# Last layer of a graph network: 256 by 256 buckets, parts summed by the matmul, edge one-hots of eight tiles in one comparison

## The reference

```python
E, N, D, H = 200000, 6250, 32, 32
h = jnp.maximum(_layernorm(x, axis=-1), 0.0)
x = x + _L0_gnn_ref(h, edge_index, edge_attr_3, ...)      # three spline convolutions
h = jnp.maximum(_layernorm(x, axis=-1), 0.0)
# the last layer, inputs = h, e = edge_weight1
ex1 = e * x[src]
ex2 = e * x[dst]
mi = jnp.zeros_like(x).at[dst].add(ex1)
mo = jnp.zeros_like(x).at[src].add(ex2)
h = jnp.concatenate([mi, mo, x], axis=1)
h = jnp.tanh(h @ W1 + b1)      # four dense layers with tanh
```

## Time and profile before

| | us |
|---|---|
| median of 3 runs | 11384.52 |
| lowest, highest | 11377.37, 11390.43 |
| profiled execution: span | 11351.5 |
| median minus span | 33.0 |
| stretch of the last layer's loop | 2450 |

### The profile page before, as it was taken

The page is one execution under the profiler, slowest core; times in us unless marked ns, Lnnn a source line. Parts: engine busy times, 40 slices in busy tenths (PEclk is TensorE's granted clock), DMA queues, the critical chain, the costliest instruction groups (busy, mean ns, idle before and its releaser), DMA issues. The chain is left out here.

```text
span 11351.5 us, 410865 instructions
## 1 busy us (share of the span) xinstructions
PE 8343.0 (73%) x149059; PEld 7488.9 (66%) x149060; DVE 7972.5 (70%) x18151; ACT 4364.6 (38%) x11249; POOL 6850.3 (60%) x6842
## 2 busy tenths in 40 slices
PE   6666666666574566565679959898987788888888
PEld 6566655555463555555568847777776688888886
DVE  5577777776574444444458848888887788888887
ACT  0010000000352333333346624444444566666665
POOL 0277777777334777777777717777775334343333
PEclk6555555555555787787789969999999777777777
DMA  1033333332102333333332212222221344444432
GB/s 39 15 75 67 68 68 67 67 68 61 23 9 62 112 111 111 111 115 109 115 103 82 77 29 62 62 62 62 62 62 52 111 127 126 127 126 128 126 129 96
DMA packets 825177, 932.53 MB, mean 82 GB/s; under 512 B 336620, under 2 KB 581924, under 8 KB 824590
## 3 DMA queue, kind: packets, MB, share of 16 engines
q1 hardware_dynamic: 641290, 726.84, 22.9%
q0 software_dynamic: 183808, 204.63, 7.2%
HBM read 610.68 MB, written 134.61 MB: 66 GB/s over the span
## 5 line engine op out<-in xcount | busy, mean ns | idle before, releaser
L765 POOL DMA_INDIRECT edges_by_rank<-rank_stage,rank_idx x1568 | 1821.5, 1162 | 505.2 <-issue 475.8
L1427 POOL DMA_INDIRECT c_near_ranked<-h_rows,c_idx x1568 | 1664.9, 1062 | 477.7 <-issue 477.1
L1552 ACT ACTIVATE c_products<-c_pa 125x512 f32<-125x512 f32 x2368 | 1222.6, 603 | 1794.7 <-PE c_pa L1596 1778.7
L1879 POOL DMA_INDIRECT edges_b<-c_send_rows,c_send_idx x1184 | 1310.1, 1106 | 396.1 <-issue 355.0
L1596 PE MATMUL c_pa<-c_near_apart,c_basis 32*125 32x128 f32 x18944 | 744.9, 294 | 1013.5 <-DVE c_near_apart L1515 911.3
L289 PE MATMUL acc_s<-hot_col,hot_row 128*123 128x78 f16 x3136 | 757.0, 410 | 956.2 <-ACT start_table L721 839.9
L2527 PE MATMUL acc_mi_mo<-msg,hot_e 128*128 128x32 bf16 x11328 | 1364.5, 191 | 115.1 <-DVE hot_e L2406 99.8
L1596 PEld LDWEIGHTS c_pa<-c_near_apart,c_basis 32*125 32x125 f32 x18944 | 638.1, 195 | 1132.2 <-issue 1132.2
L289 PEld LDWEIGHTS acc_s<-hot_col,hot_row 128*123 128x123 f16 x3136 | 718.8, 320 | 990.7 <-issue 853.6
L2527 PE MATMUL acc_mi_mo<-msg_rest,hot_e 128*128 128x32 bf16 x11328 | 1338.0, 182 | 0.0
L2527 PE MATMUL acc_mi_mo<-msg_low,hot_e 128*128 128x32 bf16 x11328 | 1336.9, 182 | 0.0
(11 more groups left out here) (402 smaller groups left out, 21082.3 us busy)
## 6 DMA issues: line engine op xcount, KB each, us to landing
own_d<-hparts SPq DMA_DIRECT2D x1888, 96.0 KB
rows<-local_rows SPq DMA_DIRECT2D x472, 256.0 KB, 3.9
hi_rows_in<-hi_rows SPq DMA_DIRECT2D x392, 256.0 KB
c_dst_rows_in<-dst_rows SPq DMA_DIRECT2D x148, 512.0 KB
near_by_rank<-c_near_ranked SPq DMA_DIRECT2D x98, 768.0 KB
rows_both<-hi_rows SPq DMA_DIRECT2D x196, 196.0 KB
near_h<-c_near_h SPq DMA_DIRECT2D x74, 512.0 KB
c_near<-near_h SPq DMA_DIRECT2D x148, 256.0 KB, 2.7
```

Source lines behind the costliest of these rows:

```text
L765: pool.indirect_dma_start(g.ranked, bass.IndirectOffsetOnAxis(idx[:, r, q:q + 1], 0), stage[:, r, q, :], None, bounds_check=last_rank, oob ...
L1427: pool.indirect_dma_start(near[:, b, q, :], None, g.h1_rows, bass.IndirectOffsetOnAxis(idx[:, b, q:q + 1], 0), bounds_check=last_node, oob ...
L1552: last = act.activation(by_round[:, half, r, rnd], pa[0:K3, r, 0:TR * P].rearrange("p (f e) -> p f e", f=width), ACT.Copy)
L1879: pool.indirect_dma_start(g.edges_b, bass.IndirectOffsetOnAxis(sending.idx[:, n, q:q + 1], 0), sending.rows[:, n, q, :], None, bounds_chec ...
```

## The change

Target blocks have 256 nodes as source blocks have: 25 x 25 = 625 buckets. The worst case then needs NT = 2192 tiles, 274 chunks of 8, and `chunks_for` no longer rounds to pairs of 16. The table holds two column offsets per tile, ready for use.

In the last layer both sides have 2 blocks of 128 nodes. The gather runs 12 matmuls of 32 columns per tile instead of 6 of 96: the three parts are accumulated into the same 32 columns, so the bank holds all 8 tiles of a chunk and VectorE's reduction is gone. VectorE multiplies by the weights straight from the bank and also takes off the upper halves; GpSimd has nothing to do. The edge one-hots of 8 tiles and one side are made by one comparison of two tensors, `local` (the numbers of the edges, 8 tiles side by side) and `numbers` (the node numbers, each 8 times), in float16 with the tile innermost. The layout is [node, tile], so `add_up` reads its stationary operand with a step of 8 elements. There are 12 matmuls per tile in `add_up` instead of 18. All buffers hold whole chunks, doubled. TensorE gathers one half of a chunk (4 tiles), then adds up one half of the chunk before it, twice per chunk. In sorting, the one-hot of the target block has 27 entries instead of 14.

```diff
-SRC_SB, DST_SB = 256, 512
-SRC_SHIFT, DST_SHIFT = 8, 9
+SRC_SB, DST_SB = 256, 256
+SRC_SHIFT, DST_SHIFT = 8, 8
...
-    step = 2 * CH
-    return -(-tiles // step) * 2
+    return -(-tiles // CH)
...
-ND1 = ND + 1
+ND1 = NBLK * P // DST_SB + 1
...
+            st.add(dve.tensor_scalar(block_of[:, :, 0], count_b[:, :], float(DST_SB // P * F), None, ALU.mult))
+            st.do(dve.tensor_scalar(block_of[:, :, 1], count_a[:, :], float(SRC_SB // P * F), None, ALU.mult))
...
-        hot_e = sb1("hot_e3", [P, 2, G, DST_SB + SRC_SB], BF16)
+        hot_e = sb1("hot_e3", [P, 2, 2, DST_SB, SH], BF16)
+        numbers, local = sb1("node_numbers3", [P, DST_SB, SH], F16), sb1("local_nodes3", [P, 2, NT], F16)
...
+                with sp.Fori(0, TURNS - 1) as i:
+                    for half in range(2):
+                        sp.wait_ge(s_hot, i * 2 + (half + 1))
+                        sp.wait_ge(s_source, i * 2 + (half + 1))
+                        bring_rows(i + 1, half)
+                        sp.wait_ge(s_gat, i * 4 + (half + 1) * 2)
+                        bring_blocks(i + 1, half)
...
+                def edge_hots(i, half, side):
+
+                    dve.tensor_tensor(hot_e[:, half, side, :, :],
+                                      local[:, side, ds(i * (2 * SH) + half * SH, SH)].unsqueeze(1)
+                                      .to_broadcast([P, DST_SB, SH]), numbers[:, :, :], ALU.is_equal)
...
+                def chunk(i, half, first, follows):
+                    if not first:
+                        dve.wait_ge(s_used, i * 2 + (half - 1))
+                    times_weight(i, half, 0)
+                    for side in range(2):
+                        edge_hots(i, half, side)
+                    if follows:
+                        dve.wait_ge(s_row[1 - half], i * 32 + (half + 1) * 32)
+                        for j in range(NJ):
+                            hot = node_hot(1 - half, j)
+                        hot.then_inc(s_hot, 1)
+                    times_weight(i, half, 1)
+                    split_rest(i, half)
+                    split_low(i, half)
...
+                def gather(i, half, h, waits):
+
+                    if waits:
+                        pe.wait_ge(s_read, i * 4 + (half * 2 + h))
+                    for q in range(h * Q, (h + 1) * Q):
+                        for side, hot, own in ((0, hot_s, own_s), (1, hot_d, own_d)):
+                            at = (q * 2 + side) * F
+                            for n in range(NJ * 3):
+                                last = pe.matmul(pg[:, at:at + F], hot[:, half, n // 3, q * P:(q + 1) * P],
+                                                 own[:, half, q, n * F:(n + 1) * F],
+                                                 start=(n == 0), stop=(n == NJ * 3 - 1))
                     last.then_inc(s_gat, 1)
...
+                                    last = pe.matmul(acc[:, ds(cols[q * 2 + side] + (col + j * F), F)],
+                                                     hot_e[:, half, side, j * P:(j + 1) * P, q],
+                                                     part[:, half, q, side * F:(side + 1) * F],
+                                                     start=False, stop=True, skip_group_check=True)
...
+                def chunk(i, half, last):
+
+                    ready(i, half)
+                    cols = blocks_of(last, 1 - half)
+                    for h in range(2):
+                        gather(i, half, h, True)
+                        if h == 0:
+                            pe.wait_ge(s_low, i * 2 + half)
+                        add_up(last, 1 - half, h, cols)
```

More of the change, by code:

```diff
@@ L2299, in second_layer @@
         acc = c_ps.enter_context(nc.psum_tensor("acc_mi_mo", [P, 7 * 512], F32))
[L2301 to L2305 removed]
+        own_d = sb1("own_d3", [P, 2, SH, NJ * 3 * F], BF16)
@@ L2319, in _, with bring_rows @@
             def _(sp):
[L2320 removed]
+                def bring_rows(i, half):
                     for kind in range(2):
                         sp.dma_start(rows[:, half, kind, :],
[L2323 to L2332 removed]
@@ new lines, in _ @@
+                dve.tensor_copy(numbers[:, :, :], g.iota16[:, :].unsqueeze(2).to_broadcast([P, DST_SB, SH]))
+                for side, column in ((0, 1), (1, 0)):
+                    last = dve.tensor_copy(local[:, side, :], g.edges[:, :, column])
+                last.then_inc(s_ready, 1)
+                dve.wait_ge(s_ready, 1)
+                dve.wait_ge(s_row[0], 32)
+                for j in range(NJ):
+                    hot = node_hot(0, j)
+                hot.then_inc(s_hot, 1)
+                chunk(0, 0, True, True)
@@ L2420, in _ @@
+                chunk(0, 1, True, True)
+                with dve.Fori(1, TURNS - 1) as i:
+                    chunk(i, 0, False, True)
+                    chunk(i, 1, False, True)
+                chunk(TURNS - 1, 0, False, True)
+                chunk(TURNS - 1, 1, False, False)
             @block.scalar
             def _(act):
-                def take_blocks(n, b):
-                    both = load_values(nc, ACTE, g.table_b[0:1, ds(n * G, G)], NA * 16 - 1)
-                    for q in range(G):
-                        a = both[q] >> 4
-                        last = act.activation(own_s[:, b, q, :], hparts[:, ds(a * (NJS * 3 * F), NJS * 3 * F)], ACT.Copy)
-                    last.then_inc(s_own, 1)
@@ L2487, in _ @@
+                act.wait_ge(s_minus, 1)
+                for half in range(2):
+                    act.wait_ge(s_row[half], 32)
+                    sources(0, half)
+                with act.Fori(1, TURNS) as i:
+                    for half in range(2):
+                        act.wait_ge(s_row[half], i * 32 + 32)
+                        act.wait_ge(s_gat, i * 4 + (half - 1) * 2)
+                        sources(i, half)
             @block.tensor
@@ L2535, in two_chunks @@
-                def two_chunks(i, more):
-                    for m in range(2 * NPAIR):
-                        if m + AHEAD < 2 * NPAIR or more:
-                            gather(i, m + AHEAD)
-                        if m % 4 == 0:
-                            both = load_values(nc, PE, g.table_b[0:1, ds(i * (2 * SH) + 2 * m, 8)], NA * 16 - 1)
-                        add_up(i, m, both)
-                for m in range(AHEAD):
-                    gather(0, m)
-                with pe.Fori(0, LOOP - 1) as i:
-                    two_chunks(i, True)
@@ new lines, in chunk @@
+                def chunk(i, half, last):
[6 more added lines that the diff above has]
+                        add_up(last, 1 - half, h, cols)
+                ready(0, 0)
+                for h in range(2):
+                    gather(0, 0, h, h > 0)
+                chunk(0, 1, 0)
@@ L2550, in second_layer @@
+                with pe.Fori(1, TURNS) as i:
+                    chunk(i, 0, i - 1)
+                    chunk(i, 1, i)
+                cols = blocks_of(TURNS - 1, 1)
+                pe.wait_ge(s_low, NC)
+                for h in range(2):
+                    add_up(TURNS - 1, 1, h, cols)
         bufs.close()
```

266 lines of the change are left out of this document (77 added, 189 removed).

## The result

| | us |
|---|---|
| kernel before, median of 4 (lowest, highest) | 11380.94 (11377.21, 11390.43) |
| changed kernel, median of 4 (lowest, highest) | 11494.99 (11491.21, 11505.03) |
| ratio, 95% interval | 1.0102 [1.0089, 1.0114] |
| forecast | 11,560 (11,050 to 11,830), slower |

The changed kernel is 1.0% slower, 114 us. The profiled execution is its longest of the four, 11505.03 us with a span of 11503.2.

The account below looks back on a forecast made before the run. TensorE was to bound the last loop: 2.6 + 1.3 + 0.3 + 5.3 = 9.5 us a chunk, 274 chunks +153 us, +24 outside, so +177 on 11384.5: 11,560 us, range 11,050 to 11,830.

Parts of the forecast that it names:

- 8.94 us: Last loop: time per chunk at which 274 chunks would equal the present 2450 us; 8.85 with the side costs.
- adding up: TensorE's chunk in the last layer: 96 matmuls of `add_up` at 55 ns, slowed by the step of 8 elements, 5.3 us.
- table load and waits: TensorE's chunk: 16 numbers at 80 ns, 1.3 us at the chunk's head, plus four waits estimated at 0.3 us.
- Not covered: Claim that TensorE's table load, 1.3 us at the head of each chunk, runs beside no other TensorE work.
- What lies beside it: Last loop: VectorE 6.0 us a chunk, ScalarE 6.4, SyncE 6.6, all hidden below 9.5; if TensorE were free, about 7.6.
- load of 8 numbers 0.6: SyncE's table load per chunk in the last loop, taken as 0.6 us of its 6.6 us sum.
- the rival: The step costs nothing: adding up 3.2 to 4.1 us, chunk about 8.0, 11,150 us, faster; chance 0.20.
- Outside the loop: Stages beside the last loop: transposes +8, loading edges +4, `numbers` and `local` +7, placing loop +5, counting loop 0; sum +24.
- The placing loop: Sorting stage: hangs on GpSimd, the 13 more one-hot entries stay below it; +5 us by contention.
- 33 us outside the span: Time counted beyond the profiled span of 11351.5 us, giving the 11384.5 us to which +177 was added.
- The lost width: Rival for TensorE's weight loads, named "Width lost": slower and outside the range of 11,050 to 11,830; chance 0.20.
- the forecast case: Matmuls of `add_up` at 46 to 65 ns, own range 11,330 to 11,830 us, mostly slower; chance 0.60.

Follow-up runs that it names:

- weights_contiguous: Changed kernel with the weight loads of `add_up` reading 128 neighbouring elements of `hot_e` instead of every eighth (sums not the reference's): 11326.53 us, ratio 0.9976.
- two_numbers: Changed kernel with TensorE reading 2 table numbers a chunk instead of 16, used for all eight tiles (sums in wrong blocks): 11409.08 us, ratio 1.0034.
- neighbour_loads: Changed kernel with edge one-hots grouped by four tiles, SyncE and ScalarE reading 16 neighbouring table numbers instead of 8 with a step of 2: 11219.54 us, ratio 0.9867.
- weights_step4: Changed kernel with the weight loads of `add_up` reading every fourth element of `hot_e` instead of every eighth (sums not the reference's): 11329.02 us, one run.
- weights_step16: Changed kernel with the weight loads of `add_up` reading every sixteenth element of `hot_e` instead of every eighth (sums not the reference's): 11513.42 us, one run.

## Why the prediction was right, and where its terms were off

**Sign and size.** Forecast +177, measured +152 from profile to profile and +114 between medians. The mechanism was the one forecast: 16% more tiles at a TensorE chunk that does not fall below 8.94 us, because `add_up` reads its weights with a step of 16 bytes.

**The chunk.** Forecast 9.5, measured 9.33 over the loop. Term by term:

| term | forecast | measured |
|---|---|---|
| gather | 96 x 27 ns = 2.6 | 27 ns, 2.6 |
| adding up | 96 x 55 ns = 5.3 | 61 ns, 5.9 |
| table load and waits | 1.3 + 0.3 | TensorE still for 0.6 to 0.85 |

The column rate of wide matmuls carried over to narrow ones: 80 ns for 96 columns before, 27 ns for 32 now, both at a granted clock of 0.50. No run shows the 55 ns that the forecast takes for a matmul of `add_up`; it was my estimate. In its place the runs showed 61 ns at a step of 8 and a clock of 0.50, and 35 ns with neighbours. The mis-sized term is the table load with its waits: 1.6 us forecast, 0.62 in the mean measured. The load takes 1.11 us (forecast 1.3, by 80 ns a number; 16 numbers take less than twice what 8 take), and about half of it runs beside matmuls that are still queued: it starts at 10005.9, the last matmul at 10006.09. "Not covered" held for the kernel before, 0.63 us in each of 237 pieces for a load of 0.64. The two errors, +0.6 and -0.8 to -1.0, nearly cancel, and that is luck.

The clock stands in the traces as a share, in records of 0.50 and 1.00. "1.2 GHz" stands for 0.50, where four gather matmuls of 96 columns of the kernel before take 0.32 us (10000.87 to 10001.19), 1.2 columns a ns; "2.4 GHz" stands for 1.00, where the same four take 0.17 us (9986.89 to 9987.06), 2.3 columns a ns.

**What lies beside it.** VectorE's 2048-element comparison: 1.21 forecast, 1.216 measured. The upper bound of 4.4 for two is 4096 elements at the 1.07 ns by which the float32 readings of 512 and 112 elements differ, (691 - 264) / 400; no run shows a cycle. `hot_d` 0.48 instead of 0.67, with GpSimd idle. VectorE is at 57%, as forecast (60%). The sums of SyncE and ScalarE were wrong: "load of 8 numbers 0.6" is 1.67 us, and on ScalarE 1.8 were left out, and what holds the chunk is a ring through both and TensorE, not the longest of them: 8.64 and not 7.6. It cost the forecast nothing, since TensorE was slower still. But it made the rival wrong: had the step been free, the time would have been 11,326 and not 11,150. weights_contiguous is that rival, and it shows that without the cost of the step the change would have gained 0.2%.

**Outside the loop.** Forecast +24, measured +45. Transposes +8 forecast, +9 measured. The placing loop is the step that failed: +5 "by contention" against +37 from profile to profile, +25 in the mean of all profiles; the width alone made the kernel before 43 us slower. I saw GpSimd as the bound and concluded that work on other engines stays under it. It did stay under it, and the transfers became longer all the same (1185 ns in the mean against 1162). `numbers`, `local` and the loads: 11 forecast, some 1 measured.

**"33 us outside the span"** were none: in every run with both numbers, the time exceeds the span by 1.8 us (11505.03 and 11503.2). The profiled execution of before was 31 us shorter than the median of three runs that the forecast starts from, and that is the rest of the 33. The forecast comes out the same, since it starts from the median of before, as it should; only the name of the term was wrong.

**The lost width** has a chance of 0.20 in the forecast, as slower and outside its range. No run shows a width of a weight load. What the runs show at a step of 8 is loads of 173 ns, 61 ns from start to start, and 11,495 us, inside the range. The 46 to 65 ns of the forecast case were my bounds; 61 lies between them.

## What to carry to other kernels

When a layout is turned to suit one engine, look at which engine reads it next and whether that one is the bound: here VectorE won 0.8 us a chunk that it had to spare and TensorE paid 2.5. A 16-bit stationary operand of 128 columns could be read here with a step of 4 elements at nearly no cost, not with 8 (loads of 104 ns with neighbours, 118 at 4, 173 at 8); grouping four tiles instead of eight keeps the batched comparison and turns 1.0% slower into 0.2% faster. Before counting on a freed engine, follow the ring through the issuing queues with their register loads, over as many chunks as the buffers allow: two small loads with a step of 2 were worth 128 us, and with the source one-hots moved to the idle VectorE the same kernel is 2.4% faster than before.

## What the runs showed of the hardware that I had not expected

- Loads of table numbers into registers: on TensorE 2 numbers 537 ns (two_numbers), 8 neighbours 644 (before), 16 neighbours 1107 (changed kernel); on SyncE 4 neighbours 303 (before), 16 neighbours 977 (neighbour_loads), 8 with a step of 2 1666 (changed kernel); on ScalarE 16 neighbours 1068 (neighbour_loads), 8 with a step of 2 1794 (changed kernel). On both, 8 with the step took longer than 16 without.
- 128-column bfloat16 weight loads: one per 35 ns with a step of 1 or 4 elements (weights_contiguous, weights_step4), one per 61 ns with 8 (changed kernel), one per 62 with 16 (weights_step16).
- With 27 instead of 14 columns on VectorE and TensorE, 1568 indirect transfers of GpSimd took 1184 ns in the mean against 1162 and 1171 in two profiles without, their median unchanged.
- Granted clock of the last loop, 9000 to 11000: 0.50 with the slow weight loads (changed kernel, weights_step16, two_numbers), 0.70 to 0.72 in the runs with steps of 1 and 4, though the latter leave TensorE still for longer (2.6 us a chunk in weights_contiguous against 0.6).
- Over the placing loop the recorded clock read 1.00 in the profile of the changed kernel and 0.50 in that of the kernel before, with 302 and 300 ns for the same matmul (L746).
